# Twelve weight halves in place of eight in the first search's GpSimd work, and the last sequence stored in two pieces

## The chip, the cores and the metric

One core of a Trainium2 chip. The metric is the device time of one launch in microseconds (us), the median of several runs.

## The reference

Four sequences x[b] of 512 rows by 512 columns. Step one picks, per sequence, the 5120 largest entries of a 512 x 512 matrix and adds a mask of ones to x. Step two is one transformer layer with modulation from `cond` (16 heads of 128, hidden width 2048).

```python
adj = s[b] * cond[b] * softmax(x[b], axis=-1) / sqrt(512)   # diagonal set to -inf
x = x + mask_of_largest(adj, 5120)
ada = cond @ ada_w + ada_b                  # shift1, scale1, gate1, shift2, scale2, gate2
x1 = ln(x) * (1 + scale1) + shift1
q, k, v = split(x1 @ qkv_w + qkv_b)
x = x + gate1 * (softmax(q k^T / sqrt(128)) v @ out_w + out_b)
x2 = ln(x) * (1 + scale2) + shift2
x = x + gate2 * (gelu(x2 @ ffn_w1 + b1) @ ffn_w2 + b2)
```

## The kernel before

**Precision by splitting.** Each product in float32 is done as three matmuls in fp32r: an operand is kept as a high part (a cast) and a low part (value minus high part), and `mm3` (L1153 to L1155) adds high x high, high x low and low x high. The weights are cut into 48 halves of 128 x 1024. Each is loaded raw once into one of two slots of `wraw` (L382), split into high and low parts, used, and saved split to a scratch tensor in DRAM (L374, L376). From the second sequence on, and for the halves called `PRE` already in the first, the split form is loaded back (1 MB each) into one of four places of `w`.

**Sequences.** `sequence(b)` runs for b = 0 to 3: value, query and key projections, 16 heads of attention, output projection (units 0 to 3), layer norm, first MLP layer (units 4 to 7), second MLP layer (units 8 to 11); a unit is two halves. Between its matmuls, sequence b also carries the search for the 5120 largest entries of sequence b + 1. Only the search of sequence 0 has nothing to lie under. It takes the first 97 us: 32 bisection steps in which DVE (L829) and ACT (L609) count and PE adds up, then the ranking `topk_mask` (DVE L915, L921, L923: a scan and two passes over 128 x 2048), the first layer norm (L930 to L949), transposes on PE (L1182), and `ln_hi` on ACT (L632, L634), which writes `xT`, the operand of the first projection.

**GpSimd in the first search.** Weight halves are handled in the order of the list `ORDER`; k is a place in it. GpSimd (POOL) splits k = 0 to 3 straight into `w` (`split_early`, L546 and L538), then the halves of `PRE` on three "desks" (`split_on_desk`, L556 cast and L558 subtraction). The desks are not memory of their own: desks 0 and 1 are the two halves of `xT`, desk 2 is `qk`, all idle until the first layer norm is applied. A desk is written again once its save has landed (`desk_saved`). Then `finish_modulation` (L565, L569, L572) completes the modulation vectors. ACT waits for `ada_ready` and then for all of `desk_saved` before `ln_hi`:

```python
            act_e.wait_ge(ada_ready, 1)
            for i in range(DESKS):
                act_e.wait_ge(desk_saved[i], 16 * len(range(i, len(PRE), DESKS)))
            ln_hi(0, ada1[:, 0:C], ada1[:, C:2 * C])
```

**SP's queue.** All weight transfers are issued by SP in program order. `load_raw` waits until half k - 2 is split (`w_ready`), issues the raw load of k, then the save of k - 2. After the desk halves SP waits for `xm_ready` (DVE L923) and loads the next x (L430). In sequence 0 the halves of units 6, 7 and 8 come by `load_ahead` (L390) as soon as PE has freed their place; halves outside `PRE` are split in the sequence, the cast by ACT (`split_hi`, L647), the subtraction by POOL (`split_lo`, L538).

**The end.** `mlp_add` (L1060) adds the last layer's columns to `x2`, 128 columns at a time; after columns 256 to 383 it signals `y2_added`, after the last 128 `out_ready`, and `store` (L439) writes 1 MB. The program ends when the stores have landed.

Of the kernel before, what the change touches and what calls it, by code (L numbers as in the profile page):

```python
# [44 lines left out]
P = 128  # L45
B, T, D = 4, 512, 512
# [10 lines left out]
NHALF = 48  # L57
# [63 lines left out]
def v_half(q, j):  # L121

    return j if q == 0 else 4 + 6 * (q - 1) + j
# [11 lines left out]
def unit_half(unit, j):  # L135


    return 22 + j if unit == 0 else NQKV + 2 * unit + j
# [15 lines left out]
TURN, USES = turns()  # L154


PRE = tuple([v_half(1, 0), v_half(1, 1)] + [unit_half(u, j) for u in (6, 7, 8) for j in range(2)])
EARLY = 4
ORDER = [n for n in range(EARLY)] + list(PRE) + [n for n in range(EARLY, NHALF) if n not in PRE]
AT = {n: k for k, n in enumerate(ORDER)}  # L160
AHEAD = EARLY + len(PRE)
DESKS = 3


def before_in_place(n, among):

    return sum(m in among for m in range(n) if PLACE[m] == PLACE[n])
# [12 lines left out]
def is_first(b):  # L180

    return isinstance(b, int) and b == 0


def block_kernel(nc, x, cond, weights, ada_w, cols, out):
    ctx = ExitStack()
    with ctx:
        here = [(nc.sbuf_base + 31) // 32 * 32]

        def at(name, shape, dt, offset):  # L190
            return nc.alloc_sbuf_tensor_at(name, shape, dt, offset=offset)
# [38 lines left out]
        x2 = at("x2", [P, NT, D], F32, v_at + 16384)  # L230
# [52 lines left out]
        def sem(name):  # L283
            return ctx.enter_context(nc.semaphore(name))
# [20 lines left out]
        y2_done, y2_gated, y2_back, out_ready = (sem("y2_done"), sem("y2_gated"), sem("y2_back"),  # L305
                                                 sem("out_ready"))
# [8 lines left out]
        y_added, y2_added = sem("y_added"), sem("y2_added")  # L315
        out_stored = sem("out_stored")
# [3 lines left out]
        STORE_CREDIT = 16  # L320
        Y2_CREDIT = C
# [6 lines left out]
        def seq(view, b):  # L328
            return view[b] if isinstance(b, int) else view[bass.ds(b, 1)].rearrange("a p n -> (a p) n")

        def wait_apart(eng, signal, value):


            eng.wait_ge(signal, value)
            eng.sem_inc(waits_met, 1)
# [3 lines left out]
        def desk(k):  # L339

            turn = (k - EARLY) % DESKS
            if turn == 2:
                return qk[:, :, :, :].rearrange("p a s t -> p (a s t)").rearrange("p (s n) -> p s n", s=2)
            at = turn * 2 * HALF
            return xT[:, :, :, :].rearrange("p a c t -> p (a c t)")[:, at:at + 2 * HALF]\
                .rearrange("p (s n) -> p s n", s=2)

        def w_credit(place):

            return USES[place] - sum(PLACE[n] == place for n in PRE)  # L350

        def w_place(n):

            region, half = PLACE[n]
            return w[:, region, :, half * HALF:(half + 1) * HALF].bitcast(F32)

        def w_wait(eng, b, n):

            if is_first(b) and n in PRE:
                eng.wait_ge(w_in[PLACE[n]], 16 * (w_credit(PLACE[n]) + before_in_place(n, PRE) + 1))  # L360
            elif is_first(b):
# [6 lines left out]
        def _(sp):  # L368
            def save_split(k):

                n = ORDER[k]
                sp.wait_ge(w_ready, k + 1)
                if n in PRE:
                    sp.dma_start(scratch[n], desk(k).bitcast(F32)).then_inc(desk_saved[(k - EARLY) % DESKS], 16)  # L374
                else:
                    sp.dma_start(scratch[n], w_place(n)).then_inc(w_saved[PLACE[n]], 16)  # L376

            def load_raw(lo, hi):
                for k in range(lo, hi):
                    if k >= 2:  # L380
                        sp.wait_ge(w_ready, k - 1)
                    sp.dma_start(wraw[:, k % 2, :], weights[ORDER[k]]).then_inc(raw_in[k % 2], 16)  # L382
                    if k >= 2:
                        save_split(k - 2)

            def load_ahead(n, freed, count):

                wait_apart(sp, freed, count)
                sp.wait_ge(w_saved[PLACE[n]], 16 * before_in_place(n, ORDER[:EARLY] + ORDER[AHEAD:]))
                sp.dma_start(w_place(n), scratch[n]).then_inc(w_in[PLACE[n]], 16)  # L390
# [38 lines left out]
            def load_x(b):  # L429
                sp.dma_start(rank, seq(x_seq, b)).then_inc(xn_in, 16)  # L430
                row = cond[b:b + 1, :] if isinstance(b, int) else cond[bass.ds(b, 1), :]
                sp.dma_start(tb[:, :], row.to_broadcast([P, T])).then_inc(tb_in, 16)

            def load_x_again(b):
                sp.dma_start(xr[:, :, :].rearrange("p i d -> p (i d)"), seq(x_seq, b)).then_inc(xr_in, 16)

            def store(b):
                wait_apart(sp, out_ready, b + 1)
                sp.dma_start(seq(out_seq, b), x2[:, :, :].rearrange("p i d -> p (i d)"))\  # L439
                    .then_inc(out_stored, 16)  # L440

            def first_sequence():
                load_raw(2, AHEAD + 2)
                wait_apart(sp, xm_ready, 1)
                load_x(1)
                for i in range(DESKS):
                    sp.wait_ge(desk_saved[i], 16 * len(range(i, len(PRE), DESKS)))
                for n in PRE:
                    if n in (v_half(1, 0), v_half(1, 1)):
                        load_ahead(n, v_done, QUAD)  # L450
                load_raw(AHEAD + 2, AT[unit_half(3, 0)])
                wait_apart(sp, pt_done, H * NT)
                load_x_again(1)
                load_raw(AT[unit_half(3, 0)], AT[unit_half(9, 0)] + 2)
                for u in (6, 7, 8):
                    for half in range(2):
                        load_ahead(unit_half(u, half), f_done, 4 * (u - 5))
                load_raw(AT[unit_half(9, 0)] + 2, NHALF)
                save_split(NHALF - 2)
                save_split(NHALF - 1)  # L460
                for place in PLACES:
                    sp.wait_ge(w_saved[place], 16 * w_credit(place))

            def sequence(b, last=False):
                load_v(b, 0)
                load_qk(b, 0)
                load_qk(b, 1)
                store(b - 1)
                if not last:
                    wait_apart(sp, xm_ready, b + 1)  # L470
                    load_x(b + 1)
                for h in range(2, H):
                    if h % QUAD == 2 and h < 14:
                        load_v(b, h // QUAD + 1)
                    if h == 14:
                        load_unit(b, 0)
                    load_qk(b, h)
                load_unit_half(b, 1, 0)
                load_unit_half(b, 1, 1)
                load_unit_half(b, 2, 0)  # L480
                if not last:

                    wait_apart(sp, pt_done, b * (H * NT) + H * NT)
                    load_x_again(b + 1)
                load_unit_half(b, 3, 0)
                load_unit_half(b, 2, 1)
                load_unit_half(b, 3, 1)
                for u in range(4, NUNIT):
                    load_unit(b, u)
# [8 lines left out]
            for c in range(C):  # L498
                sp.dma_start(adaw[:, c, :], ada_w[c * P:(c + 1) * P, :]).then_inc(ada_in, 16)
            load_x_again(0)  # L500
            first_sequence()
            for b in range(1, B - 1):
                sequence(b)
            sequence(B - 1, last=True)
            store(B - 1)
            sp.wait_ge(out_stored, 16 * B + STORE_CREDIT)


        @block.gpsimd
# [972 lines left out]
```

## Time and profile before

| | us |
|---|---|
| median of 3 runs | 1692.48 |
| lowest, highest | 1692.33, 1693.62 |
| the profiled execution | 1692.08 |
| its span | 1690.1 |
| PE busy | 1621.2 (96%) |
| DVE busy | 1160.2 (69%) |
| ACT busy | 858.1 (51%) |
| POOL busy | 157.5 (9%) |
| granted TensorE clock, mean | 0.999 |

The span is what the profiler recorded, the profiled execution's own time is 1.98 us longer. Busy time is time in which an engine had an instruction in work; an engine's share is its part of the span. Times in the rows below are us from the start of the span, unless a unit stands there.

### The profile page before, as it was taken

What the parts mean: (1) busy time and instruction counts of PE and PEld (TensorE: products, weight loads), DVE (VectorE), ACT (ScalarE), POOL (GpSimd) and SP (SyncE); (2) the same over time, 40 slices, a digit from 0 to 9 for tenths busy, and PEclk for the clock granted to TensorE, in tenths of its full rate; (3) what the DMA queues carried; (4) which work ended last, traced back from release to release, by engine and by line L of the source; (5) the groups of instructions that cost most, each with busy time, mean ns of one, the idle gap of its engine ahead of it and who ended that gap; (6) DMA issues with size and microseconds to landing.
All of it is one profiled execution on the core that took longest, in us unless ns stands there. A gap on an engine that the chain in (4) does not pass through costs nothing.

```text
span 1690.1 us, 22637 instructions
## 1 busy us (share of the span) xinstructions
PE 1621.2 (96%) x8317; PEld 1357.5 (80%) x8317; DVE 1160.2 (69%) x2556; ACT 858.1 (51%) x1623; POOL 157.5 (9%) x93
## 2 busy tenths in 40 slices
PE   2879999999999999999999999999999999999998
PEld 2868888888788888888778888888878888888887
DVE  7867877767776877776774887776775666665421
ACT  4546666655835455552743555554571545544240
POOL 4612221214040000000000000000000000000000
PEclk9999999999999999999999999999999999999999
DMA  9913444447565223224446133134354331332453
GB/s 343 336 59 115 169 136 155 159 144 255 187 249 215 115 76 125 100 100 150 156 193 241 64 125 125 50 125 150 150 193 181 125 125 54 129 117 93 157 199 124
DMA packets 63853, 256.32 MB, mean 152 GB/s; under 512 B 4352, under 2 KB 4480, under 8 KB 60800
## 3 DMA queue, kind: packets, MB, share of 16 engines
q1 hardware_dynamic: 63456, 254.56, 40.7%
q8 instruction: 66, 1.08, 0.2%
q14 instruction: 43, 0.35, 0.1%
q10 hardware_dynamic: 288, 0.33, 0.1%
HBM read 200.34 MB, written 54.53 MB: 151 GB/s over the span
## 4 chain that ended last, share of the span: by engine, by line
PE 89%; DVE 6%; ACT 3%; issue 1%; DVEq 1%; DMA 0%; SPq 0%
PE bank L1153 25%; PE bank L1155 24%; PE bank L1154 24%; PE bank L1252 7%; PE bank L1415 2%; DVE tb L829 1%; PE bank L1278 1%; PE bank L1320 1%; PE bank L1315 1%; PE bank L1316 1%; DVE prob L1006 1%; PE bank L1200 1%; PE bank L1182 1%; ACT prob L704 1%; PE bank L1204 1%
## 5 line engine op out<-in xcount | busy, mean ns | idle before, releaser
L1153 PE MATMUL bank<-xT,w 128*128 128x512 f32 x704 | 279.9, 398 | 0.5 <-POOL w L538 0.5
L704 ACT ACTIVATE prob<-bank,nbias 128x512 f32<-128x512 f32 x256 | 176.6, 690 | 201.9 <-DVE nbias L1003 201.9
L1155 PE MATMUL bank<-xT,w 128*128 128x512 f32 x704 | 274.5, 390 | 0.0
L1154 PE MATMUL bank<-xT,w 128*128 128x512 f32 x704 | 274.2, 390 | 0.0
L1153 PE MATMUL bank<-act,w 128*128 128x512 f32 (+1 forms) x576 | 217.6, 378 | 0.8 <-DVE act L967 0.8
L1155 PE MATMUL bank<-act,w 128*128 128x512 f32 (+1 forms) x576 | 211.1, 367 | 0.0
L1154 PE MATMUL bank<-act,w 128*128 128x512 f32 (+1 forms) x576 | 210.8, 366 | 0.0
L1014 DVE TENSOR_TENSOR probT<-bank,probT 128x512 fp32r<-128x512 f32 x256 | 158.6, 682 | 24.7 <-ACT probT L714 24.6
L997 DVE TENSOR_REDUCE rowmax<-bank 128x1 f32<-128x512 f32 x256 | 174.8, 683 | 0.0
L1155 PEld LDWEIGHTS bank<-xT,w 128*128 128x128 f32 x704 | 132.1, 188 | 27.9
L1153 PEld LDWEIGHTS bank<-xT,w 128*128 128x128 f32 x704 | 132.1, 188 | 26.1 <-POOL w L538 0.9
L1154 PEld LDWEIGHTS bank<-xT,w 128*128 128x128 f32 x704 | 132.3, 188 | 25.1
L714 ACT CAST probT<-bank 128x512 fp32r<-128x512 f32 x256 | 131.1, 603 | 17.5 <-PE bank L1252 17.5
L538 POOL TENSOR_TENSOR w<-wraw,w 128x1024 fp32r<-128x1024 f32 x40 | 103.6, 2594 | 296.0 <-ACT w L647 295.6
L1006 DVE TENSOR_SCALAR prob<-prob,rinv 128x512 f32<-128x512 f32 x256 | 125.4, 490 | 5.4 <-issue 0.5
L967 DVE SCALAR_TENSOR_TENSOR act<-bank,small,act 128x512 fp32r<-128x512 f32 x64 | 48.0, 750 | 116.0 <-ACT act L723 116.0
L1252 PEld LDWEIGHTS bank<-ident,prob 128*128 128x128 f32 x1024 | 114.8, 141 | 14.1 <-DVE prob L1006 7.4
L1252 PE MATMUL bank<-ident,prob 128*128 128x128 f32 x1024 | 122.8, 273 | 2.7 <-DVE prob L1006 2.7
L1155 PEld LDWEIGHTS bank<-act,w 128*128 128x128 f32 x576 | 108.6, 188 | 18.1
L1153 PEld LDWEIGHTS bank<-act,w 128*128 128x128 f32 x576 | 108.7, 189 | 17.8 <-DVE act L967 2.5
L1154 PEld LDWEIGHTS bank<-act,w 128*128 128x128 f32 x576 | 108.8, 189 | 15.5
L967 DVE SCALAR_TENSOR_TENSOR qk<-bank,small,qk 128x512 fp32r<-128x512 f32 x128 | 95.1, 749 | 31.5 <-ACT qk L695 22.3
(151 smaller groups left out, 3065.4 us busy)
## 6 DMA issues: line engine op xcount, KB each, us to landing
w<-split_weights SPq DMA_DIRECT2D x152, 1024.0 KB, 5.3
split_weights<-w SPq DMA_DIRECT2D x40, 1024.0 KB, 6.1
wraw<-weights_in SPq DMA_DIRECT2D x48, 512.0 KB, 4.2
adaw<-ada_w_in SPq DMA_DIRECT2D x4, 1536.0 KB, 13.3
split_weights<-xT SPq DMA_DIRECT2D x6, 1024.0 KB, 7.6
xr<-x_in SPq DMA_DIRECT2D x4, 1024.0 KB, 5.7
out<-x SPq DMA_DIRECT2D x4, 1024.0 KB, 4.4
adj<-x_in SPq DMA_DIRECT2D x3, 1024.0 KB, 7.0
```

The costliest lines, as they stand in the source:

```text
L538: nc.gpsimd.tensor_tensor(w[:, region, 1, span], wraw[:, k % 2, :], w[:, region, 0, span].bitcast(F32), ALU.subtract)\
L704: nc.scalar.activation(prob[:, i, :], bank[i][:, :], ACT.Exp, bias=nbias[:, i:i + 1], scale=SCALE, accum_out=rowsum[:, i:i + 1]).then_inc( ...
L714: nc.scalar.copy(probT[:, 0, j, :], bank[j][:, :]).then_inc(pt_hi, 1)
L967: return V.scalar_tensor_tensor(dst, src, bias, hi.bitcast(F32), ALU.add, ALU.subtract)
L997: V.reduce_max(rowmax[:, i:i + 1], bank[i][:, :], AX.X)
L1006: V.tensor_scalar(prob[:, i - 1, :], prob[:, i - 1, :], rinv[:, i - 1:i], None, ALU.mult)\
L1014: V.tensor_tensor(probT[:, 1, j, :], bank[j][:, :], probT[:, 0, j, :].bitcast(F32), ALU.subtract).then_inc(pt_lo, 1)
L1153: pe.matmul(dst, w_hi_ap, x_hi_ap, start=first, stop=False)
L1154: pe.matmul(dst, w_hi_ap, x_lo_ap, start=False, stop=False)
L1155: return pe.matmul(dst, w_lo_ap, x_hi_ap, start=False, stop=last)
L1252: ins = pe.transpose(bank[j][:, i * P:(i + 1) * P], prob[:, i, j * P:(j + 1) * P], ident[:, :])
L1415: ins = pe.matmul(bank[0][:, m * B:(m + 1) * B], adaw[:, c, m * P:(m + 1) * P], small[:, c0 + c * B:c0 + (c + 1) * B], start=c == 0, stop= ...
```

## The change

`PRE` gets four more halves, those of units 9 and 10, so that 12 halves (k = 4 to 15) go over the desks during the first search. In sequence 0 these four are no longer split between ACT and POOL but loaded back in split form. The last sequence is stored in two pieces: columns 0 to 383 at `y2_added`, columns 384 to 511 at `out_ready`. Lines behind the new function `store_last` stand 7 or 8 higher in the changed kernel; all line numbers in this text are those of the kernel before unless it says otherwise.

```diff
--- before.py
+++ after.py
@@ -154,7 +154,7 @@
 TURN, USES = turns()
 
 
-PRE = tuple([v_half(1, 0), v_half(1, 1)] + [unit_half(u, j) for u in (6, 7, 8) for j in range(2)])
+PRE = tuple([v_half(1, 0), v_half(1, 1)] + [unit_half(u, j) for u in (6, 7, 8, 9, 10) for j in range(2)])
 EARLY = 4
 ORDER = [n for n in range(EARLY)] + list(PRE) + [n for n in range(EARLY, NHALF) if n not in PRE]
 AT = {n: k for k, n in enumerate(ORDER)}
@@ -439,6 +439,12 @@
                 sp.dma_start(seq(out_seq, b), x2[:, :, :].rearrange("p i d -> p (i d)"))\
                     .then_inc(out_stored, 16)
 
+            def store_last(signal, columns):
+
+                wait_apart(sp, signal, B)
+                sp.dma_start(out[B - 1].rearrange("(p i) d -> p i d", p=P)[:, :, columns], x2[:, :, columns])\
+                    .then_inc(out_stored, 16)
+
             def first_sequence():
                 load_raw(2, AHEAD + 2)
                 wait_apart(sp, xm_ready, 1)
@@ -451,11 +457,12 @@
                 load_raw(AHEAD + 2, AT[unit_half(3, 0)])
                 wait_apart(sp, pt_done, H * NT)
                 load_x_again(1)
-                load_raw(AT[unit_half(3, 0)], AT[unit_half(9, 0)] + 2)
-                for u in (6, 7, 8):
+                load_raw(AT[unit_half(3, 0)], NHALF)
+                for u in (6, 7, 8, 9):
                     for half in range(2):
                         load_ahead(unit_half(u, half), f_done, 4 * (u - 5))
-                load_raw(AT[unit_half(9, 0)] + 2, NHALF)
+                for half in range(2):
+                    load_ahead(unit_half(10, half), y2_done, Y2_CREDIT + 1)
                 save_split(NHALF - 2)
                 save_split(NHALF - 1)
                 for place in PLACES:
@@ -502,8 +509,9 @@
             for b in range(1, B - 1):
                 sequence(b)
             sequence(B - 1, last=True)
-            store(B - 1)
-            sp.wait_ge(out_stored, 16 * B + STORE_CREDIT)
+            store_last(y2_added, slice(0, D - P))
+            store_last(out_ready, slice(D - P, D))
+            sp.wait_ge(out_stored, 16 * (B + 1) + STORE_CREDIT)
 
 
         @block.gpsimd
```

The order on POOL in the first search, from the last two desk halves to the first split of sequence 0. `xT` and `qk` are the desks, `ada` the modulation vectors. Before:

```order
L556 CAST xT<-wraw 128x1024
L558 TENSOR_TENSOR xT<-wraw,xT 128x1024
L556 CAST xT<-wraw 128x1024
L558 TENSOR_TENSOR xT<-wraw,xT 128x1024
L565 TENSOR_TENSOR ada<-ada,small 128x96
L569 TENSOR_SCALAR ada<-ada 128x16 x2
L572 COPY ada_76<-ada 128x8
L538 TENSOR_TENSOR w<-wraw,w 128x1024 x2
```

Now, from the same two desk halves on (L564, L566 are L556, L558 of before; L573 to L580 are L565 to L572):

```order
L564 CAST xT<-wraw 128x1024
L566 TENSOR_TENSOR xT<-wraw,xT 128x1024
L564 CAST qk<-wraw 128x1024
L566 TENSOR_TENSOR qk<-wraw,qk 128x1024
L564 CAST xT<-wraw 128x1024
L566 TENSOR_TENSOR xT<-wraw,xT 128x1024
L564 CAST xT<-wraw 128x1024
L566 TENSOR_TENSOR xT<-wraw,xT 128x1024
L564 CAST qk<-wraw 128x1024
L566 TENSOR_TENSOR qk<-wraw,qk 128x1024
L573 TENSOR_TENSOR ada<-ada,small 128x96
L577 TENSOR_SCALAR ada<-ada 128x16 x2
L580 COPY ada_76<-ada 128x8
```

Four casts and four subtractions stand between the last desk half of before and the modulation.

SP's queue at the same place, from the save of desk half k = 9 on. Each pair is a raw load and the save of the half two places earlier; `adj<-x_in` is the load of the next x. Before:

```order
L374 DMA split_weights<-qk 128x2048
L382 DMA wraw<-weights_in 128x1024
L374 DMA split_weights<-xT 128x2048
L382 DMA wraw<-weights_in 128x1024
L374 DMA split_weights<-xT 128x2048
L430 DMA adj<-x_in 128x2048
L432 DMA tb<-cond_in 128x512
```

Now, from the save of k = 11 on, the last one of before:

```order
L374 DMA split_weights<-xT 128x2048
L382 DMA wraw<-weights_in 128x1024
L374 DMA split_weights<-qk 128x2048
L382 DMA wraw<-weights_in 128x1024
L374 DMA split_weights<-xT 128x2048
L382 DMA wraw<-weights_in 128x1024
L374 DMA split_weights<-xT 128x2048
L382 DMA wraw<-weights_in 128x1024
L374 DMA split_weights<-qk 128x2048
L430 DMA adj<-x_in 128x2048
L432 DMA tb<-cond_in 128x512
```

Four saves from the desks (and the raw loads beside them) have come in ahead of the load of the next x.

SP's queue at the end of the program, from the weight loads of the last sequence on. Before:

```order
L439 DMA out<-x_66 128x2048
L395 DMA w<-split_weights 128x2x1024 x44
L439 DMA out<-x_66 128x2048
```

Now (L445 is `store_last`):

```order
L395 DMA w<-split_weights 128x2x1024 x44
L445 DMA out<-x_66 512x1x384
L445 DMA out<-x_66 512x1x128
```

One transfer of 128 runs has become one of 512 runs of 384 elements and one of 512 runs of 128.

## Rows read from the trace of the kernel before

**Rows 1.** The page, busy time of each engine over the whole span.
```profile
PE 1621.2 (96%) x8317; PEld 1357.5 (80%) x8317; DVE 1160.2 (69%) x2556; ACT 858.1 (51%) x1623; POOL 157.5 (9%) x93
```

**Rows 2.** PE's waits for POOL, us 95 to 560: us in total, times, longest.
```profile
PE bank L1153 <- POOL w L538: 0.5, 1, 0.5
```

**Rows 3.** Timeline, us 84 to 106: start, duration, engine, line, operation [idle before].
```profile
87.17 4.42 DVE L915 TENSOR_TENSOR_SCAN adj<-eqm 128x2048 f32<-128x2048 bf16 x1
91.79 2.35 DVE L921 SCALAR_TENSOR_TENSOR eqm<-adj,need,low 128x2048 bf16<-128x2048 f32 x1
94.22 2.29 DVE L923 TENSOR_TENSOR xm<-xr,eqm 128x2048 f32<-128x2048 f32 x1
104.10 0.78 ACT L632 ACTIVATE xT<-bank,ada 128x512 fp32r<-128x512 f32 x1 [4.08 <-PE bank L1182]
105.02 0.47 PE L1200 MATMUL bank<-w,xT 128*128 128x512 f32 x1 [0.71 <-ACT xT L632]
```

**Rows 4.** Timeline of POOL (GpSimd) after the first search's desk work.
```profile
73.64 1.04 POOL L556 CAST xT<-wraw 128x1024 fp32r<-128x1024 f32 x1 [0.28 <-DMA wraw<-weights_in]
74.76 2.35 POOL L558 TENSOR_TENSOR xT<-wraw,xT 128x1024 fp32r<-128x1024 f32 x1
89.38 2.36 POOL L565 TENSOR_TENSOR ada<-ada,small 128x96 f32<-128x96 f32 x1 [12.27 <-ACT ada L808]
91.91 4.71 POOL L569 TENSOR_SCALAR ada<-ada 128x16 f32<-128x16 f32 x2 [0.17 <-issue]
```

**Rows 5.** Timeline of SP's DMA issues, us 77 to 78.
```profile
77.14 0.33 SPq L382 DMA_DIRECT2D wraw<-weights_in  x1
77.51 0.45 SPq L374 DMA_DIRECT2D split_weights<-xT  x1
```

**Rows 6.** Line L382: landing of the raw load issued at 77.14.
```profile
DMA to landing us min/median/max: 5.5/5.5/5.5
```

**Rows 7.** Line L376: landing of the save issued at 213.7.
```profile
DMA to landing us min/median/max: 6.0/6.0/6.0
```

**Rows 8.** Timelines of POOL and DVE where both work, two places.
```profile
52.12 1.78 POOL L556 CAST qk<-wraw 128x1024 fp32r<-128x1024 f32 x1 [3.58 <-DMA wraw<-weights_in]
50.72 2.29 DVE L904 TENSOR_TENSOR low<-low,adj 128x2048 f32<-128x2048 f32 x1
475.75 8.79 POOL L538 TENSOR_TENSOR w<-wraw,w 128x1024 fp32r<-128x1024 f32 x2 [6.63 <-ACT w L647]
478.15 4.14 DVE L921 SCALAR_TENSOR_TENSOR eqm<-adj,need,low 128x2048 bf16<-128x2048 f32 x1 [0.15 <-issue]
482.37 4.33 DVE L923 TENSOR_TENSOR xm<-xr,eqm 128x2048 f32<-128x2048 f32 x1
```

**Rows 9.** Timeline of PE: same matmuls in sequences 0 and 1, second MLP layer.
```profile
475.08 0.18 PE L1172 MATMUL bank<-n_eq,minus_half 128*128 128x1 f16 x1
870.66 0.18 PE L1172 MATMUL bank<-n_eq,minus_half 128*128 128x1 f16 x1
501.19 1.91 PE L1182 MATMUL bank<-ident,z 128*128 128x128 f32 x16
896.75 1.91 PE L1182 MATMUL bank<-ident,z 128*128 128x128 f32 x16
```

**Rows 10.** Line L1422: least, median and longest of its 17 matmuls.
```profile
L1422 PE MATMUL bank<-w x17: 389/519/763, 96.7 to 102.2; 128*128 128x512 f32 x17
```

**Rows 11.** Tail: last addition (DVE), last store (SP), its landing.
```profile
1685.06 0.69 DVE L1060 TENSOR_TENSOR x<-x,bank 128x512 f32<-128x512 f32 x1 [0.75 <-PE bank L1278]
1685.84 0.35 SPq L439 DMA_DIRECT2D out<-x  x1
DMA to landing us min/median/max: 3.9/3.9/3.9
```

**Rows 12.** DMA view, us 1685 to 1690.1, in 40 slices of 0.1275 us.
```profile
GB/s 0 0 0 0 0 0 0 0 0 0 0 0 0 835 193 450 578 0 900 129 514 514 129 835 64 514 514 0 900 129 514 514 0 0 0 0 0 0 0 0
```

**Rows 13.** Line L495: landing of its four 256 KB loads.
```profile
DMA to landing us min/median/max: 3.2/4.5/4.8
```

## The prediction

> **What bounds the kernel now.** I read four views in this order: the page for the bound, PE's waits for where splits of weights cost anything, the timelines of all engines around the end of the first search, and the timelines of the tail. The page [rows 1] says that PE is busy 96% of the span, so over most of it work on POOL, ACT or the DMA queues costs nothing unless PE waits for it. Two stretches are different. Up to 105 us PE has no large work: the path goes through the ranking on DVE (a scan and two passes), the layer norm, and `ln_hi` on ACT, which starts at 104.10; the first projection follows at 105.02 [rows 3]. And behind the last addition at 1685.06 only the store is left, 3.9 us from issue to landing [rows 11]. Whatever starts later than 104.10 or lands sooner than that store shows in the time one for one.
>
> **What the removed splits are worth: nothing.** In the whole of sequence 0 PE waits for a split by POOL once, for 0.5 us [rows 2]. The reader can test the second MLP layer directly, because sequence 1 runs the same matmuls with its weights loaded split, as units 9 and 10 now will be in sequence 0. From the rank matmul to the transposes of the next layer norm, sequence 0 takes 501.19 - 475.08 = 26.11 us and sequence 1 takes 896.75 - 870.66 = 26.09 us [rows 9]. POOL's four subtractions and ACT's four casts are hidden under PE there, and so are the eight loads that replace raw load and save. If that cover were gone, the two stretches would differ. Term: 0.0 us, at most 0.5 us gained [rows 2].
>
> **What the longer desk work costs.** Each desk half takes POOL 3.5 us: the cast starts at 73.64, the subtraction at 74.76 and lasts 2.35, and SP issues the next raw load at 77.14 [rows 4, 5]. Before, this was the end (k = 11); POOL then stood idle until 89.38 and closed the modulation with three short instructions by 96.6 [rows 4]. Now k = 12 to 15 follow.
> 1. Raw 12 was loaded before, too; it was issued as k = 10 was done, 3.8 us ahead of raw 13 (77.14, landing 5.5 later at 82.6 [rows 5, 6]), so it lands near 78.8. So k = 12 runs from 78.9 to 82.4 and k = 13 from 82.8 to 86.3.
> 2. Raw 14 goes out at 82.4 and raw 15 at 86.3. With the same 5.5 us they land at 87.9 and 91.8.
> 3. Now POOL meets the scan (87.17 to 91.59) and the two passes behind it [rows 3]. Such pairs have been seen. The cast at 52.12 took 1.78 us in place of 1.04; it ended 0.9 us after DVE's L904 (50.72 + 2.29) had [rows 4, 8]. Two subtractions from 475.75 took 8.79 us in place of 4.7, and DVE's L921 and L923 took 4.14 and 4.33 in place of 2.35 and 2.29 [rows 3, 8]. That is what taking turns gives: POOL waits for the scan, DVE's first pass for POOL, POOL for that pass, and so on. L565 and L569, with 96 and 16 elements, fit in: they ended just behind the scan and behind each of the two passes [rows 3, 4].
> 4. Taking turns: cast 14 until 92.5; L921 92.5 to 94.9 (it would have started at 91.79); subtraction 14 until 97.2; L923 97.2 to 99.5; cast 15 until 100.4; subtraction 15 until 102.8. L923 ends 3.0 us later than before (96.51), and half 15 is split at 102.8.
> 5. Three things are late then. DVE's chain alone would let `ln_hi` start at 104.1 + 3.0 = 107.1. The modulation, no longer blocked, ends about 1 us after 102.8. The save of k = 15 is issued by SP behind raw 17, 0.4 us after 102.8 (the distance of the two issues in [rows 5]), so at 103.2; a save in a quiet queue lands 6.0 us after its issue [rows 7]: 109.2. ACT waits for that save, since desk 2's save counts in `desk_saved`, so `ln_hi` starts at 109.3: 5.2 us later than 104.10. Queued behind the waiting ACT are `ln_hi` and all of sequence 0; PE, DVE and POOL wait for it. SP itself is free, and its load of the next x (now at 103.7) is wanted only under head 0.
>
> The bounds of this term: a save that lands in 5.5 us, as a raw load does in a filled queue [rows 6], gives 4.7. If the save waits for 1.5 us of other transfers it gives 6.7. I take 5.2, because at 103 us the queue holds only raw 17, as it does in row 7. The Trainium skill ("SBUF — State Buffer", section "SBUF: two separate sides") says that the port pair which GpSimd shares with VectorE is an exclusive lock that the first comer holds for the whole instruction. By that rule GpSimd would also stop a DVE instruction with two SBUF inputs, as step 4 has it, and it speaks against this change; rows 8 agree, with 4.14 us for 2.35.
>
> **What the split store gains.** In the last store data flow from 1686.7 to 1689.0 [rows 12], 2.3 of its 3.9 us. Of the 1 MB, 256 KB remain for the last piece; the first 768 KB go out at 1679, under PE's last matmuls, and are long done. At the same rate a quarter takes 0.6 us, a gain of 1.7. The nearest row for a transfer of this size is the first load of x, 3.2 us to landing at best [rows 13], a gain of 0.7. The piece is cut into 512 runs in place of 128, which lengthens issue and packets, so I take the middle: 1.2. The Trainium skill ("DMA: Bandwidth & Descriptors", section "Specifications") puts the smallest piece at line rate at 512 bytes, which is just the run here. By that page alone the sum would use 1.7; no row shows a store with such runs.
>
> **The sum.** +5.2 - 1.2 + 0.0 = +4.0 us. On the profiled execution's 1692.08 that is 1696.1; it stands 0.4 below the median 1692.48, so against the median I predict 1696.5.
>
> **Rivals.**
> *The save lands in time (not slower).* If POOL and DVE did not block each other, or DVE's passes always went first and cost POOL only little, k = 15 would start with raw 15 at 91.9, be split at 95.4, and its save issued at 95.8 would land at 101.8. The place is ACT's wait ahead of `ln_hi`; the point from which it decides is a split of k = 15 by 104.1 - 6.0 - 0.4 = 97.7. Then only the tail counts: 1692.48 - 1.2 = 1691.3. For it: the cast at 52.12 did not slow L904 [rows 8]. Against it: L921 and L923 lost 1.8 and 2.0 us at 478 to 487 [rows 3, 8], and POOL must pass exactly these two here. Chance 0.14.
> *PE slows after a longer pause.* PE finishes its transposes at 104.3 now and starts projecting after 0.7 us [rows 3]. In the changed kernel the transposes move by 3.0 and the projection by 5.2, so the pause is about 2.9 us. After the 9.3 us pause ahead of L1422 its 17 matmuls took 519 ns in the median and 389 at least [rows 10], so a slow restart costs 17 x 0.13 = 2.2 us and gives 1698.7. Against it: this pause is a third as long, and the granted clock on the page stays at 9 tenths or more (the 2.4 GHz level) throughout. Chance 0.10. The Trainium skill ("TensorE: Matmul & The Clock Gate", section "HAM oscillation — how this bites in real kernels") describes kernels in which pauses for data send the engine back to its lower clock; that would be this case.
> *The removed splits pay after all.* Sequence 0 would have to gain 2 us or more beside the tail, with the save in time: 1692.48 - 1.7 - 0.5 - 2 = 1688.3. Rows 9 leave no room for it. Chance 0.04.
>
> **How the numbers follow.** The forecast has 0.72. Its own range is 1692.48 + 4.7 - 1.7 = 1695.5 to 1692.48 + 6.7 - 0.7 = 1698.5. A measurement of this kernel can tell about 0.2%, 3.4 us, from no change, so the line stands at 1695.9: I give 0.16 of the 0.72 to its lower edge (same) and 0.56 to slower. The slow restart adds 0.10 to slower. The save in time is same, 0.14; the paying splits are faster, 0.04. Slower 0.66, same 0.30, faster 0.04. The range for 8 in 10 takes the forecast and the slow restart whole and goes part of the way towards the save in time: 1692.5 to 1699.5.
>
> **What would show it.** In the changed profile: POOL's casts and subtractions at L564 and L566 go on to about 103 us, with the last ones longer than 1.04 and 2.35; DVE's two passes take over 3 us in at least one case; `ln_hi` starts near 109.3, later than the transposes end, and no longer releases right behind PE; stretches from there on are shifted by one constant, sequence 0's second MLP layer included; the last transfer lands about 2.7 us after its issue. I am wrong if `ln_hi` starts before 107 (the save was in time and only DVE's delay or nothing counted), if L921 and L923 stay at 2.3 us, or if sequence 0 from `ln_hi` to its end is more than 1 us shorter than before.

## The result, and the profile after

The changed kernel takes 1697.43 us in the median of 22 runs (1695.45 to 1699.64) against 1693.34 for the kernel before (22 runs, 1692.25 to 1696.94, the three known ahead of the prediction among them): a ratio of 1.0021, 95% interval 1.0015 to 1.0027. That is 3.6 us more, between 2.5 and 4.6. The prediction said 1696.5 and a range of 1692.5 to 1699.5, and gave 0.66 to "slower", which it let begin at 3.4 us. That the kernel got slower is clear of noise; whether by more than 3.4 us is not. The profiled execution took 1696.26 us, 4.2 more than the one of before.

The page after, span and busy time of each engine; PE still rules [rows 1]:

```profile
span 1694.5 us, 22647 instructions
PE 1622.7 (96%) x8317; PEld 1358.8 (80%) x8317; DVE 1158.4 (68%) x2556; ACT 854.4 (50%) x1619; POOL 160.0 (9%) x97
```

The end of the first search, timelines of DVE, ACT and PE (start, duration, engine, line, operation, idle before). Lines stand 8 higher than in [rows 3]: L923, L929 and L931 are the scan and the two passes, L640 is `ln_hi`, L1208 the first projection:

```profile
88.02 4.43 DVE L923 TENSOR_TENSOR_SCAN adj<-eqm 128x2048 f32<-128x2048 bf16 x1
92.65 4.08 DVE L929 SCALAR_TENSOR_TENSOR eqm<-adj,need,low 128x2048 bf16<-128x2048 f32 x1
96.80 2.97 DVE L931 TENSOR_TENSOR xm<-xr,eqm 128x2048 f32<-128x2048 f32 x1
108.89 0.78 ACT L640 ACTIVATE xT<-bank,ada 128x512 fp32r<-128x512 f32 x1 [5.62 <-DMA split_weights<-qk]
109.81 0.47 PE L1208 MATMUL bank<-w,xT 128*128 128x512 f32 x1 [2.17 <-ACT xT L640]
```

Both passes have grown, 2.35 to 4.08 and 2.29 to 2.97, and `ln_hi` is no longer released by PE's transposes but by the landing of the save from `qk`, the desk of half 15, for which ACT waited 5.62 us. From the start of the scan to `ln_hi` it was 104.10 - 87.17 = 16.93 us [rows 3] and is 108.89 - 88.02 = 20.87, 3.94 more. The rest of the 4.79 us lies ahead of the scan, which began 0.85 us later in this execution. 0.68 of that is DVE's L904 (here L912): it took 2.97 us in place of 2.29 beside a cast of POOL. The change did not touch that place; more of it below.

The 3.94 us can be divided by the transposes whose first part releases `ln_hi` when nothing else is late, before (L1182) and after (L1190):

```profile
102.39 1.91 PE L1182 MATMUL bank<-ident,z 128*128 128x128 f32 x16
105.73 1.91 PE L1190 MATMUL bank<-ident,z 128*128 128x128 f32 x16
```

Before, `ln_hi` followed their start by 104.10 - 102.39 = 1.71 us. At the same distance it would now have started at 107.44. So the late passes make 107.44 - 88.02 - 16.93 = 2.5 us of the 3.94, and the wait for the save 1.45.

POOL at the same place, desk halves 14 and 15 and the modulation:

```profile
87.13 1.04 POOL L564 CAST xT<-wraw 128x1024 fp32r<-128x1024 f32 x1 [0.57 <-DMA wraw<-weights_in]
88.24 6.34 POOL L566 TENSOR_TENSOR xT<-wraw,xT 128x1024 fp32r<-128x1024 f32 x1
94.53 3.10 POOL L564 CAST qk<-wraw 128x1024 fp32r<-128x1024 f32 x1
97.71 4.29 POOL L566 TENSOR_TENSOR qk<-wraw,qk 128x1024 fp32r<-128x1024 f32 x1
101.96 0.35 POOL L573 TENSOR_TENSOR ada<-ada,small 128x96 f32<-128x96 f32 x1
102.48 0.48 POOL L577 TENSOR_SCALAR ada<-ada 128x16 f32<-128x16 f32 x2 [0.17 <-issue]
```

The reader should see the turns. The subtraction from 88.24 lasts 6.34 us in place of the 2.35 of [rows 4]: it waits for the scan, which holds on until 92.45, then runs, and the first pass, whose record begins at 92.65, waits for it and ends at 96.73. (An instruction's time in these rows holds its waiting for the other engine.) The cast from 94.53 waits for that pass and the second pass for the cast. L573 and L577, 2.36 and 4.71 us in [rows 4], take 0.35 and 0.48 with no pass beside them: what they showed before was waiting. The Trainium skill ("SBUF — State Buffer", section "Who interferes with whom") says the second of the two to issue is blocked until the first has finished, whichever engine it is; by that rule both columns should stretch in turn, and the trace agrees, with 6.34 us on POOL and 4.08 on DVE.

The save of half 15, issue and landing:

```profile
102.39 0.43 SPq L374 DMA_DIRECT2D split_weights<-qk  x1
DMA to landing us min/median/max: 6.3/6.3/6.3
```

102.39 + 6.3 = 108.7, and `ln_hi` starts at 108.89. Behind it PE slowed. Busy time by stretches of 2 us; the column after POOL's is TensorE's granted clock:

```profile
108.00:110.00 2.00, 0.19 (x1) 0.22 (x2) 0.00 (x0) 1.11 (x2) 0.00 (x0) 1.00 0.99 422
110.00:112.00 2.00, 2.00 (x7) 1.57 (x7) 0.98 (x2) 2.00 (x4) 0.00 (x0) 0.68 0.68 168
112.00:114.00 2.00, 2.00 (x6) 1.54 (x6) 1.09 (x2) 2.00 (x4) 0.00 (x0) 0.50 0.00 0
114.00:116.00 2.00, 2.00 (x10) 1.65 (x9) 0.79 (x3) 0.35 (x1) 0.00 (x0) 0.97 0.02 4
```

The clock falls to 0.50, the 1.2 GHz level, about 1 us after PE has taken up work again, and is back before 116; matmuls in between take 0.63 us in place of 0.39. The pause ahead of the projection was 2.17 us; before the change it was 0.71 with the clock at 1.00. From the first projection matmul to the first one of the next step it took 113.30 - 105.02 = 8.28 us before and takes 119.72 - 109.81 = 9.91: 1.6 us more. The page cannot show such a fall: its clock row has slices of 42 us and reads 9 tenths in every one of them, after the change as before.

Second MLP layer of sequence 0: the two matmuls of [rows 9] on PE, and the two passes of [rows 8] on DVE (L921, L923, here L929, L931). Then the tail as in [rows 11, 12] (the last row in 40 slices from 1690 to 1694.5, 0.1125 us each):

```profile
480.93 0.18 PE L1180 MATMUL bank<-n_eq,minus_half 128*128 128x1 f16 x1
507.00 1.91 PE L1190 MATMUL bank<-ident,z 128*128 128x128 f32 x16
484.00 2.35 DVE L929 SCALAR_TENSOR_TENSOR eqm<-adj,need,low 128x2048 bf16<-128x2048 f32 x1 [0.15 <-issue]
486.43 2.29 DVE L931 TENSOR_TENSOR xm<-xr,eqm 128x2048 f32<-128x2048 f32 x1
```

```profile
1690.74 0.69 DVE L1068 TENSOR_TENSOR x<-x,bank 128x512 f32<-128x512 f32 x1 [0.75 <-PE bank L1286]
1691.52 0.58 SPq L445 DMA_DIRECT2D out<-x  x1
DMA to landing us min/median/max: 2.6/2.6/2.6
GB/s 0 0 0 0 0 0 0 0 0 0 0 0 0 0 0 0 0 0 0 0 0 0 0 0 73 291 305 291 291 287 291 291 192 18 0 0 0 0 0 0
```

The stretch takes 26.07 us, as the 26.11 and 26.09 of [rows 9]. With the splits gone from it, the two passes take 2.35 and 2.29 us there, where they took 4.14 and 4.33 [rows 8]. DVE gains 3.8 us and the kernel nothing, because PE is busy all the time from 472 to 492 us in both profiles.

The last transfer lands 2.6 us from its issue in place of 3.9 [rows 11]. Its 256 KB, in runs of 512 bytes, flow at some 290 GB/s. The 768 KB ahead of it, in runs of 1536 bytes, flow at some 370 in the middle of their transfer (1686 to 1688 us).

### The profile page after: what moved, and what is told of

Read it like the earlier page. It is cut to its first block, busy times and chain, and to the rows that moved or that the text cites. A ratio compares the mean times of both kernels' runs of the same rounds, so it can differ in the third digit from the quotient of the medians.

```text
span 1694.5 us, 22647 instructions
## 1 busy us (share of the span) xinstructions
PE 1622.7 (96%) x8317; PEld 1358.8 (80%) x8317; DVE 1158.4 (68%) x2556; ACT 854.4 (50%) x1619; POOL 160.0 (9%) x97
## 4 chain that ended last, share of the span: by engine, by line
PE 86%; DVE 4%; DMA 3%; ACT 3%; POOL 2%; issue 1%; DVEq 1%; POOLq 0%; SPq 0%; ACTq 0%
PE bank L1161 25%; PE bank L1163 24%; PE bank L1162 24%; PE bank L1260 7%; DMA wraw<-weights_in 2%; PE bank L1286 1%; PE bank L1328 1%; PE bank L1323 1%; PE bank L1324 1%; PE bank L1208 1%; PE bank L1212 1%; PE bank L1209 1%; POOL xT L566 1%; PE bank L1190 1%; ACT prob L712 1%
## 5 line engine op out<-in xcount | busy, mean ns | idle before, releaser
L1161 PEld LDWEIGHTS bank<-xT,w 128*128 128x128 f32 x704 | 132.1, 188 | 26.1 <-POOL w L546 0.9
L546 POOL TENSOR_TENSOR w<-wraw,w 128x1024 fp32r<-128x1024 f32 x36 | 88.7, 2466 | 306.5 <-ACT w L655 306.2
```

Source lines behind the costliest of these rows:

```text
L546: nc.gpsimd.tensor_tensor(w[:, region, 1, span], wraw[:, k % 2, :], w[:, region, 0, span].bitcast(F32), ALU.subtract)\
L1161: pe.matmul(dst, w_hi_ap, x_hi_ap, start=first, stop=False)
```

## The experiments

Most of these kernels vary by 3 to 5 us from run to run, so besides each ratio (in brackets the same in us, at 1693) I give a span inside the profile: from the start of the tie count (DVE L909, right ahead of the scan) to the start of `ln_hi`. It is 104.10 - 84.72 = 19.4 us before and 108.89 - 85.58 = 23.3 after.

**The desk work alone.** The changed kernel with the old end:

```diff
-            store_last(y2_added, slice(0, D - P))
-            store_last(out_ready, slice(D - P, D))
-            sp.wait_ge(out_stored, 16 * (B + 1) + STORE_CREDIT)
+            store(B - 1)
+            sp.wait_ge(out_stored, 16 * B + STORE_CREDIT)
```

> The twelve desk halves alone; the last sequence is stored in one piece as before. Theory (the desk work costs time at the start, the split store gives some back): ln_hi starts 4 to 5.5 us later than before, the last transfer lands 3.9 us after its issue, and the run takes 5.0 to 6.0 us more than before. Rival (the desk work is free and the split store is what costs): within 1 us of before.

Measured: 1698.77, ratio 1.0029, 1.0018 to 1.0040 (+4.9 us). Timeline rows of `ln_hi` and the first projection:

```profile
110.14 0.78 ACT L639 ACTIVATE xT<-bank,ada 128x512 fp32r<-128x512 f32 x1 [6.83 <-DMA split_weights<-qk]
111.06 0.47 PE L1207 MATMUL bank<-w,xT 128*128 128x512 f32 x1 [2.76 <-ACT xT L639]
```

Tie count to `ln_hi` 24.6 us, the save last again, PE's pause 2.76 us and the projection 9.9 us long; the store at the end lands 3.9 us after its issue, as before. The desk work costs about 5 us (3.0 to 6.8), at the lower edge of what was expected, and the rival of a free desk falls.

**The split store alone.** The kernel before with the new end and nothing else (`store_last` and its two calls, as in the change).

> Eight desk halves as before, the last sequence stored in two pieces. Theory: 1.3 us less than before (last transfer 2.6 us from issue to landing in place of 3.9), and 5 to 6 us less than the changed kernel. Rival (512 runs of 512 bytes cost what the smaller size saves): no difference from before.

Measured: 1692.39, ratio 0.9992, 0.9984 to 1.0001 (-1.4 us). The interval just touches no change, so the run times alone do not show the gain. The profile does: the last transfer lands 2.6 us after its issue, in place of 3.9. The two parts add up, 4.9 - 1.4 = 3.5 us, where together they measure 3.6, but the first is known to 1.9 us and the second to 1.4.

**The last save taken off `ln_hi`.** `ln_hi` writes `xT`, desks 0 and 1; desk 2 is `qk` and first written later:

```diff
-            for i in range(DESKS):
+            for i in range(DESKS - 1):
                 act_e.wait_ge(desk_saved[i], 16 * len(range(i, len(PRE), DESKS)))
             ln_hi(0, ada1[:, 0:C], ada1[:, C:2 * C])
...
             def qk_part(b, h):
+                if is_first(b) and h == 0:
+                    act_e.wait_ge(desk_saved[DESKS - 1], 16 * len(range(DESKS - 1, len(PRE), DESKS)))
```

> The changed kernel, but ACT waits for the saves of the desk that lies in qk only ahead of its first write to qk, not ahead of ln_hi. Theory (the wait that ends last is the save of half 15, and its pause lets TensorE's clock fall): ln_hi starts as soon as the transposes release it, near 107.5, 3.3 us later than before, the granted clock stays at 1.00 behind it, and the run takes 2.5 to 3.5 us less than the changed kernel, so 1 to 2 us more than before. Rival (DVE's late passes set it all, the save lands under them): no change against the changed kernel. Rival (the first write to qk then waits just as long): same time as the changed kernel, with an ACT wait for the save ahead of the write to qk.

Measured: 1695.00, ratio 1.0007, 0.9998 to 1.0015 (+1.2 us), 2.4 less than the changed kernel. DVE's scan and passes, and `ln_hi`:

```profile
90.16 5.75 DVE L925 TENSOR_TENSOR_SCAN adj<-eqm 128x2048 f32<-128x2048 bf16 x1
96.11 2.78 DVE L931 SCALAR_TENSOR_TENSOR eqm<-adj,need,low 128x2048 bf16<-128x2048 f32 x1
98.96 4.27 DVE L933 TENSOR_TENSOR xm<-xr,eqm 128x2048 f32<-128x2048 f32 x1
110.77 0.78 ACT L640 ACTIVATE xT<-bank,ada 128x512 fp32r<-128x512 f32 x1 [4.04 <-PE bank L1192]
```

`ln_hi` starts later than the 107.5 expected, because the tie count began at 87.71 in this execution (84.72 before), but the transposes release it. The pause is 0.71 us again and the projection 8.28 us; the first write to `qk` waits for the matmuls, not for the save. So the wait for the last save, with the slow restart behind it, was worth some 2.4 us of the changed kernel. What is left is DVE: here even the scan lost 1.3 us, to a subtraction that began first, and the passes lost 0.4 and 2.0. Together that is the whole growth from tie count to `ln_hi`, 23.1 us in place of 19.4. Its cost beside the split store is 1.2 + 1.4 = 2.6 us.

**PE's pause filled, first try.** Nine warm-up matmuls behind `transpose_z(0)`:

```diff
             transpose_z(0)
+            for i in range(9):
+                pe.matmul(bank[7][:, :], w[:, 0, 0, 0:P], w[:, 0, 0, 0:T], start=True, stop=True)
```

> The changed kernel with nine more matmuls of the warm-up kind (into bank 7, whose content is not used) between the transposes and the first projection, 2.0 us of work in PE's pause of 2.2 us. Theory (the pause costs a fall of the granted clock to 0.5 for some 3 us): the first projection's matmuls stay at 0.39 us, granted clock 1.00 in 110 to 114, and the run takes 1.5 us less than the changed kernel. Rival (the slow matmuls have another cause, such as ACT's and DVE's work on the banks beside them): matmuls of 0.63 us as before and no gain, or a loss of up to 0.3 us.

Measured: 1697.15, ratio 1.0018, 1.0009 to 1.0026 (+3.0 us). This decides nothing about the clock. In the profiled execution the search ran later against the desk work, and `ln_hi` was released by the transposes:

```profile
110.16 0.78 ACT L640 ACTIVATE xT<-bank,ada 128x512 fp32r<-128x512 f32 x1 [3.94 <-PE bank L1190]
```

There was no pause to fill, and the nine matmuls stood in the way instead: the first projection started 2.13 us after `ln_hi` (112.29) where it is 0.92 in [rows 3]. The nine matmuls come behind the transposes on PE, so they cannot have shortened `ln_hi`'s wait: with the same desk work the save ends last in one execution and DVE's chain in another.

**Ten halves.** The split-store kernel with unit 9 added to `PRE`, unit 10 split in the sequence as before.

```diff
-... for u in (6, 7, 8) for j in range(2)])
+... for u in (6, 7, 8, 9) for j in range(2)])
...
-                load_raw(AT[unit_half(3, 0)], AT[unit_half(9, 0)] + 2)
-                for u in (6, 7, 8):
+                load_raw(AT[unit_half(3, 0)], AT[unit_half(10, 0)] + 2)
+                for u in (6, 7, 8, 9):
...
-                load_raw(AT[unit_half(9, 0)] + 2, NHALF)
+                load_raw(AT[unit_half(10, 0)] + 2, NHALF)
```

> Ten desk halves (units 6 to 9), last sequence stored in two pieces. Theory (only halves 14 and 15 meet the scan and the two passes; the splits removed from the sequence are worth nothing): half 13 is split before the scan ends, DVE's passes stay at 2.35 and 2.29 us, ln_hi is released by the transposes as before, and the run takes the same as the kernel with eight halves and a split store, within 0.7 us: about 1.3 us less than before. Rival (each desk half costs its share): 1.5 to 2.5 us more than that kernel. Rival (removed splits pay in the sequence): over 0.5 us less than that kernel.

Measured: 1692.95, ratio 0.9997, 0.9988 to 1.0006 (-0.5 us). POOL's last desk half, DVE's scan and passes, and `ln_hi`:

```profile
83.67 1.04 POOL L563 CAST xT<-wraw 128x1024 fp32r<-128x1024 f32 x1 [0.20 <-DMA wraw<-weights_in]
84.78 2.35 POOL L565 TENSOR_TENSOR xT<-wraw,xT 128x1024 fp32r<-128x1024 f32 x1
90.34 4.42 DVE L922 TENSOR_TENSOR_SCAN adj<-eqm 128x2048 f32<-128x2048 bf16 x1
94.96 2.35 DVE L928 SCALAR_TENSOR_TENSOR eqm<-adj,need,low 128x2048 bf16<-128x2048 f32 x1 [0.15 <-issue]
97.39 2.29 DVE L930 TENSOR_TENSOR xm<-xr,eqm 128x2048 f32<-128x2048 f32 x1
107.08 0.78 ACT L639 ACTIVATE xT<-bank,ada 128x512 fp32r<-128x512 f32 x1 [3.90 <-PE bank L1189]
```

Half 13 ends at 87.1, the scan begins at 90.34, nothing is slowed, and tie count to `ln_hi` is 19.2 us. Two of the four added halves are free at this place, so the cost is not one per half. Against the split store alone the median is 0.6 higher and the ratios differ by 0.9 us with intervals of 1.5 to either side: no gain shows from the two splits removed, and a gain or loss of 1 us can't be told.

**GpSimd stands back.** The changed kernel, with POOL waiting for the second pass ahead of half 14:

```diff
+                if k == AHEAD - 2:
+                    pool.wait_ge(xm_ready, 1)
```

> The changed kernel, but GpSimd begins desk half 14 only when DVE's two passes are done (it waits for xm_ready). Theory (the passes are late only through GpSimd's work beside them; then the save of half 15 sets ln_hi): the scan, L921's and L923's counterparts take 4.42, 2.35 and 2.29 us again, half 15 is split 7 to 8 us after the second pass ends, its save lands 6.3 us later, ln_hi starts 6 to 7.5 us later than before relative to the start of the scan, PE's pause is over 5 us with granted clock 0.5 behind it, and the run takes 2 to 4 us more than the changed kernel. Rival (the passes are slowed by something else, the DMA traffic of the saves): they stay above 2.7 us.

Measured: 1699.69, ratio 1.0040, 1.0026 to 1.0054 (+6.8 us). Desk halves 14 and 15, the two passes, `ln_hi`, and the clock:

```profile
98.26 1.04 POOL L566 CAST xT<-wraw 128x1024 fp32r<-128x1024 f32 x1 [10.05 <-DVE xm L933]
102.81 2.39 POOL L568 TENSOR_TENSOR qk<-wraw,qk 128x1024 fp32r<-128x1024 f32 x1
93.48 2.35 DVE L931 SCALAR_TENSOR_TENSOR eqm<-adj,need,low 128x2048 bf16<-128x2048 f32 x1 [0.15 <-issue]
95.91 2.29 DVE L933 TENSOR_TENSOR xm<-xr,eqm 128x2048 f32<-128x2048 f32 x1
112.54 0.78 ACT L642 ACTIVATE xT<-bank,ada 128x512 fp32r<-128x512 f32 x1 [10.53 <-DMA split_weights<-qk]
112.00:114.00 2.00, 0.54 (x1) 0.50 (x2) 0.00 (x0) 1.46 (x3) 0.00 (x0) 0.86 0.96 403
114.00:116.00 2.00, 2.00 (x6) 1.60 (x5) 1.34 (x2) 2.00 (x4) 0.00 (x0) 0.50 0.27 96
```

The passes take 2.35 and 2.29 us again. During the first one the DMA engines are 37% busy, and they were 35% busy during the one that took 4.08 us in the changed kernel, so POOL's work slowed it and not the transfers. The price has moved to the save: tie count to `ln_hi` 26.1 us, and the granted clock at 0.50 behind a pause of over 5 us.

**The same, with the pause filled** by 24 of the matmuls above.

> As the kernel in which GpSimd stands back, with 24 matmuls of the warm-up kind (5.5 us of work, into bank 7, content not used) in PE's pause. Theory (a long pause makes the granted clock fall): first projection's matmuls at 0.39 us, granted clock 1.00, from the first to the last of the first projection about 8.3 us in place of about 10, and 1.5 us less than the kernel without them. Rival (no clock effect): the stretch takes the same in both and so do the runs.

Measured: 1698.01, ratio 1.0028, 1.0017 to 1.0040 (+4.7 us), 1.7 below its sibling. With few runs of either, none of the six here (1696.92 to 1698.74) is as slow as the fastest of the four there (1699.07). The clock column:

```profile
112.00:114.00 2.00, 2.00 (x10) 1.64 (x10) 0.80 (x2) 2.00 (x4) 0.00 (x0) 1.00 0.47 185
114.00:116.00 2.00, 2.00 (x11) 1.65 (x10) 1.27 (x2) 2.00 (x4) 0.00 (x0) 1.00 0.01 3
```

`ln_hi` waits as long (26.2 us from the tie count), but the clock stays at 1.00 and the projection takes 8.2 us in place of 9.9. So the 1.6 us behind the long pause are the clock's. For the pause of 2.17 us this was not tested by filling it; there the clock column and the matmuls of 0.63 us say the same.

**A wait that avoids the collision in the middle.** Besides the passes at the end there are L901 and L904 between the two levels of the search. In the profile of the split store alone POOL and DVE met there:

```profile
49.49 1.04 POOL L563 CAST qk<-wraw 128x1024 fp32r<-128x1024 f32 x1 [1.74 <-DMA wraw<-weights_in]
50.61 3.20 POOL L565 TENSOR_TENSOR qk<-wraw,qk 128x1024 fp32r<-128x1024 f32 x1
49.51 2.10 DVE L908 TENSOR_SCALAR low<-adj,cand 128x2048 f32<-128x2048 uint16 x1
51.68 4.27 DVE L911 TENSOR_TENSOR low<-low,adj 128x2048 f32<-128x2048 f32 x1
```

L901 and L904 (here L908, L911) take 2.10 and 4.27 us; in the profile of before they took 1.29 and 2.29, since only a cast fell there, behind L904's start [rows 8]. With eight halves, split store and

```diff
+                if k == EARLY + 2:
+                    pool.wait_ge(cand_ready, LEVEL + 1)
```

> Eight desk halves and a split store, and GpSimd begins desk half 6 only when DVE has made the low words and started the second level (cand_ready at 17), so that none of its work lies beside L901 and L904. Theory (the spread of the run times of every kernel here is the same collision in the middle of the search, 0 to 2.8 us by how the loads fall): L901's and L904's counterparts take 1.29 and 2.29 us, the runs lie within 1.5 us of each other, and the median is 0.8 to 2 us below that of eight halves with a split store. Rival (the spread comes from DMA or the launch): spread and median unchanged. Rival (half 6 held back makes the desk work end too late): ln_hi waits for a save.

Measured: 1691.46, ratio 0.9989, 0.9980 to 0.9998 (-1.9 us). Ten of its 11 runs lie between 1690.65 and 1691.83; those of the split store alone between 1690.44 and 1695.75.

```profile
48.40 2.35 POOL L567 TENSOR_TENSOR xT<-wraw,xT 128x1024 fp32r<-128x1024 f32 x1
54.43 1.04 POOL L565 CAST qk<-wraw 128x1024 fp32r<-128x1024 f32 x1 [3.68 <-DVE cand L847]
49.94 1.89 DVE L910 TENSOR_SCALAR low<-adj,cand 128x2048 f32<-128x2048 uint16 x1
51.91 2.29 DVE L913 TENSOR_TENSOR low<-low,adj 128x2048 f32<-128x2048 f32 x1
```

L904 is back at 2.29. L901 still lost 0.6 us to half 5's subtraction, which the wait doesn't hold, so that part of the theory failed. `ln_hi` is released by the transposes. This kernel is ahead of both the kernel before and the changed one. Against the split store alone its median is 0.9 lower, but the ratios differ by 0.5 us only, less than their intervals.

**The wait alone**, in the kernel before.

> The kernel before with one edit: GpSimd begins desk half 6 only when DVE has started the second level of the search. Store and number of halves as before. Theory (part of the gain of the kernel with eight halves, split store and this wait comes from the wait): 0.4 to 1.2 us less than before, L904's counterpart at 2.29 us, and all but one run in ten within 1.5 us of each other. Rival (all of that kernel's gain was the split store): median as before and a spread of 4 to 5 us as before.

Measured: 1692.55, ratio 0.9996, 0.9987 to 1.0005 (-0.7 us). The size is as expected, but the interval holds no change as well, and the runs spread over 3.7 us (1690.97 to 1694.68), so the second half of the expectation failed. The profile has POOL waiting for DVE at this place and L904's counterpart at 2.29 us, which it also took in the profile of before. That the wait is worth 0.7 us is not shown.

## Why the prediction was right, step by step

- *The removed splits are worth nothing*: right. 26.07 us against 26.11, and ten halves showed no gain over eight. (The loads added are four, not the eight that the prediction counts.)
- *Steps 1 and 2, when the raws land*: half right. Raw 14 landed 4.4 us after its issue, not 5.5, at 86.7. Cast 14 so came in ahead of the scan (87.13), and the first instruction to be blocked was the subtraction.
- *Steps 3 and 4, taking turns*: right in kind, with another order of turns. The passes lost 1.7 and 0.7 us against my 0.8 and 2.2; the second pass ended 2.4 us later against the start of the scan (11.75 against 9.34) where I had 3.0. The kernel in which POOL stands back shows that POOL is the cause.
- *Step 5, the save sets `ln_hi`*: right in this profile. Split at 102.0 (102.8 forecast), landed at 108.7 (109.2). The lateness of 4.79 us (5.2 forecast) is 3.94 by the desk work and 0.85 by an earlier part of the search, so the desk term was 1.3 too high here.
- *PE slows after a longer pause*, a rival to which I gave 0.10: it came about, on top of the forecast. It cost 1.6 us, not the 2.2 worked out from L1422, and a pause of 2.2 us was enough where I had counted on 2.9 being too short. My second argument against it, the clock row of the page, was worth nothing: that row also reads 9 tenths throughout in the kernel in which the clock fell.
- *The split store*: -1.2 forecast, 1.3 in the profile, -1.4 in the runs. Of the two bounds the middle was right. With runs of 512 bytes 290 GB/s flowed, against 1 MB in 2.3 us (455 GB/s) in [rows 12], and the issue took 0.58 us in place of 0.35. The rule of line rate from 512 bytes on that the Trainium skill gives ("DMA: Bandwidth & Descriptors", section "Specifications") would have made it 1.7; the trace does not agree with it here.
- *The sum*: +4.0 forecast, +3.6 by the ratio. By the runs the desk work alone costs 4.9, which holds the clock (5.2 forecast without it), and the split store gives 1.4. In the profile the pieces are 0.85 (search) + 3.94 + 1.63 (clock) - 1.3 (tail) = 5.1 against 4.2 measured.
- *One constant shift from `ln_hi` on*: not quite. The lateness is 4.79 us at `ln_hi`, 6.41 at the first head's transposes (136.04 against 129.63), 5.87 at the counts behind the heads (384.69 against 378.82) and 5.68 at the last addition. Of the 0.9 us that came back, 0.5 did so in the heads, where PE's waits for DVE's `prob` (L1006) ahead of the transposes sum up to 1.7 us in place of 2.2. Another 0.2 came back from there to the last addition, and 0.2 lies outside the span. Why PE waited less is not known.

So the mechanism was right, and the number was in part luck: a desk term that was 1.3 us too high in this profile and a clock term of 1.6 us that was left out nearly cancel. The 1696.5 itself stood on a median of three runs, 1692.48; with 22 runs it was 1693.34.

What I treated as fixed is a matter of phase, that is, of when POOL's pieces fall against DVE's. Of kernels with the same desk work and the same wait, the profiles of two had the save last (the changed one, the desk work alone), and one had DVE's chain last (the one with nine matmuls). The forecast's turns were one draw among several; from tie count to `ln_hi` these three cost 3.2 to 5.3 us more than before.

## What to carry to other kernels

Filling an idle engine is free only up to the point where its work meets another engine's instructions on the critical path; ask of each added piece what it will stand beside, and not how much idle time there is in sum. Work put on memory that the next stage needs (here the desks in `xT` and `qk`) ends with the landing of its save, so put that wait ahead of the first write to the very buffer; here that was worth 2.4 us. When a kernel's runs spread by more than the effect, look for a stretch inside the trace that holds the effect and not the spread.

## What the runs showed that I had not expected

- The first search varies from one execution to the next by the same collision in its middle, with or without the change. L901 and L904 together took 3.6 us in the profile of before and 6.4 in that of the split store alone, which have the same first search, by where half 6's split fell. In the 11 profiles the tie count starts between 84.6 and 87.9 us; with the time of L901 and L904 taken off, between 81.0 and 81.9 is left. How much of the spread of the run times this makes is open. The kernel that keeps POOL away from L904, with the split store, spread over 1.2 us in ten of 11 runs, but the wait alone spread over 3.7.
- A cast is enough to hold DVE up, if it begins first: L901 took 2.10 us with a cast that began 0.02 us ahead of it (49.49 and 49.51). In the changed kernel L901 began first (49.56), kept its 1.29 us, and the cast of 49.65 took 2.09 in place of 1.04.
- The tie count and the counts of the bisection (L909, L829) are not slowed: the tie count took 2.35 us before the change with POOL idle, and 2.35 after it with half 13's subtraction beside it; each count takes 1.25 us in either case.
- TensorE's granted clock fell not in the pause of 2.17 us but about 1 us after it, when PE was busy again, and cost as much as after a pause of 5.23 us (9.91 and 9.86 us for the same projection, 8.28 with the clock at 1.00).
